# A convolution and local-attention block: image 0's first two planes as plain fp32 products, with the weight preparation around them reordered

## The reference

```
perceived = depthwise 3x3 conv (3 filters per channel) of x  + b_perc      # 384 channels
hid       = gelu(w_up1 @ perceived + b_up1)                                # 256 channels, exact gelu
h         = x + w_up2 @ hid + b_up2                                        # 128 channels
q, k, v   = w_qkv @ h + b_qkv
out       = h + sum over the 3x3 neighbourhood of softmax(q.k * 128**-0.5) * v   # zero-padded borders
```

## Time and profile before

| | |
|---|---|
| median of 3 runs | 394.77 us (394.73 to 394.92) |
| the profiled execution's own time | 394.93 us |
| span in the profile | 393.1 us, granted clock 0.999 |
| busy: PE / DVE / ACT / POOL | 382.4 / 340.3 / 256.5 / 180.0 us |
| DMA | 33.98 MB, mean 86 GB/s |

### The profile page before, as it was taken

How to read it: one execution, slowest core, us unless ns; L and a number is a source line. 1 busy time by engine, 2 the same in 40 slices (tenths; PEclk the granted TensorE clock), 3 DMA queues, 4 the chain that set the end, 5 groups by cost and what they waited for, 6 DMA issues and landing times.

```text
span 393.1 us, 10470 instructions
## 1 busy us (share of the span) xinstructions
PE 382.4 (97%) x3664; PEld 359.6 (91%) x3664; DVE 340.3 (87%) x919; ACT 256.5 (65%) x542; POOL 180.0 (46%) x159
## 2 busy tenths in 40 slices
PE   5999999999999999999999999999999999999995
PEld 4999998999989999999999999999999999999874
DVE  4999999999988889888888988888898888887795
ACT  6645478929485774848477484847748484773893
POOL 5784563646445262635525263552526355132111
PEclk9999999999999999999999999999999999999999
DMA  7420301434151513325150332515033231403003
GB/s 226 183 67 3 121 2 25 139 45 170 31 187 20 171 32 65 141 39 173 25 181 14 74 131 39 173 26 175 21 71 132 39 107 26 121 12 85 3 27 135
DMA packets 56313, 33.98 MB, mean 86 GB/s; under 512 B 47200, under 2 KB 48096, under 8 KB 56288
## 3 DMA queue, kind: packets, MB, share of 16 engines
q1 hardware_dynamic: 56000, 33.61, 30.3%
q10 hardware_dynamic: 288, 0.05, 0.1%
HBM read 19.86 MB, written 8.39 MB: 72 GB/s over the span
## 4 chain that ended last, share of the span: by engine, by line
PE 83%; DVE 11%; issue 2%; DMA 1%; ACT 1%; POOL 0%; DVEq 0%; ACTq 0%
PE m_ps L484 45%; PE work L539 10%; PE s_ps L609 9%; PE work L583 7%; PE s_ps L592 6%; PE s_ps L578 2%; PE s_ps L575 2%; PE s_ps L576 2%; DVE t L970 1%; DMA wp<-w_perc 1%; DVE tlo L977 1%; DVE h_around L1238 1%; DVE h_lo L987 1%; DVE s_ps L1012 1%; PE work L562 1%
## 5 line engine op out<-in xcount | busy, mean ns | idle before, releaser
L484 PE MATMUL m_ps<-thi,whi 128*128 128x256 f32 x558 | 158.9, 285 | 0.9 <-DVE ru_sb L1058 0.8
L484 PE MATMUL m_ps<-thi,wlo 128*128 128x256 f32 x558 | 155.5, 279 | 0.0
L484 PE MATMUL m_ps<-tlo,whi 128*128 128x256 f32 x558 | 154.3, 276 | 0.0
L484 PEld LDWEIGHTS m_ps<-thi,whi 128*128 128x128 f32 x558 | 104.8, 188 | 4.3 <-issue 1.0
L484 PEld LDWEIGHTS m_ps<-tlo,whi 128*128 128x128 f32 x558 | 105.6, 189 | 0.6
L484 PEld LDWEIGHTS m_ps<-thi,wlo 128*128 128x128 f32 x558 | 104.9, 188 | 0.0
L1404 POOL TENSOR_TENSOR hid_lo<-hid,hid_hi 128x1024 fp32r<-128x1024 f32 x30 | 72.2, 2406 | 27.9 <-ACT hid_hi L741 21.4
L1381 POOL TENSOR_TENSOR fc<-xp 128x512 f32<-128x512 f32 x16 | 21.3, 1333 | 98.3 <-DVE tlo L977 91.8
L731 ACT ACTIVATE hid<-y,b1eff 128x1024 f32<-128x1024 f32 x31 | 35.7, 1152 | 33.1 <-DVE y L1081 23.1
L715 ACT CAST thi<-t 128x1024 fp32r<-128x1024 f32 (+1 forms) x32 | 25.1, 832 | 48.6 <-DVE t L970 48.5
L807 ACT ACTIVATE p_sb<-p_sb,negmax 128x101 f32<-128x101 f32 x128 | 46.8, 369 | 6.2 <-DVE negmax L1111 6.1
(11 more groups left out here) (156 smaller groups left out, 765.6 us busy)
## 6 DMA issues: line engine op xcount, KB each, us to landing
xp<-x_planes SPq DMA_DIRECT2D x16, 640.0 KB, 5.3
xr<-x_rows SPq DMA_DIRECT2D x16, 512.0 KB, 4.1
out<-o_sb SPq DMA_DIRECT2D x28, 256.0 KB, 4.0
pt<-ptc SPq DMA_DIRECT2D x140, 32.0 KB, 1.9
pt<-ptc SPq DMA_DIRECT2D x28, 28.0 KB, 1.9
out<-y SPq DMA_DIRECT2D x3, 256.0 KB, 2.5
w1T<-w SPq DMA_DIRECT2D x1, 384.0 KB, 3.6
out<-y SPq DMA_DIRECT2D x2, 128.0 KB, 2.4
```

Of the source, the lines that this page charges most:

```text
L484: last = pe.matmul(bank[:, col + first:col + end], a[:, j, dy, half * P:(half + 1) * P], c[:, par, T_PLACE[j], first + by:end + by], start ...
```

## The change

For image 0, planes 0 and 1 of both halves are computed by plain fp32 matmuls (`whole_products`) straight from `t` and the unsplit weights: plane 0 before `small_weights`, plane 1 after it. The remaining eight units follow plane by plane in a new order (plane 5, then 3, 2, 4 for half 0, then for half 1). The three products after `small_weights` (L471) are gone, and `keep_busy` multiplies a zeroed tile instead of w1T, four times. DVE does tap column 0, then image 0's transform, then tap column 2; ACT makes the diagonals before its part of tap column 2. The low parts of weights 0 and 1, needed from image 1 on, go to POOL, the folded bias to ACT, `z_base` to image 1's body on DVE. `weff` 1 and 3 live elsewhere, and image 0 has other banks. The w1T transfer is cut in three, and image 0's planes are loaded from ACT's queue after the filters and the identity, no more from SP's after w1T. DVE makes image 1's first `tlo` part ahead of `combine(0, 0)`, the second after `finish_y(0, 0)`; POOL's `differences(2, 0)` waits until the first half's `y` of image 0 is made; the second half's `hid_lo` of image 0 is made by DVE, no more by POOL. At the end, `turn_p(n, 1)` comes after one row of copies instead of two, and one `add_h` comes after the copies.

```diff
-            sp.dma_start(w1T[:, :, :].rearrange("p m d -> p (m d)"), w1_c).then_inc(first_in, 16)
-            load_planes(0, 0)
+            for m in range(3):
+                sp.dma_start(w1T[:, m, :], w1_c[:, m * HID:(m + 1) * HID]).then_inc(w1_in[m], 16)
...
 # PE
-                    pe.matmul(work[:, 2, HID + 8:CH], w1T[:, 0, 0:P], w1T[:, 0, 8:HID], start=True, stop=True)
+                    pe.matmul(work[:, 2, S:S + WINDOW], pt[:, 0, 0, 0:P], pt[:, 0, 1, :], start=True, stop=True)
...
-                pe.wait_ge(first_in, 16)
-                keep_busy(5)
+                pe.wait_ge(zeroed, 5)
+                keep_busy(4)
+                for m in range(3):
+                    pe.wait_ge(w1_in[m], 16)
...
-                for _ in range(3):
-                    last = pe.matmul(m_ps[:, 2, S:CH], w1T[:, 0, 0:P], w1T[:, 0, 0:S], start=True, stop=True)
-                last.then_inc(warm_done, 1)
+            def whole_products(half, j, w):
+                b, col = M_PLACE[j]
+                bank = m_bank(0, half, b)
+                for k, dy in enumerate((1, 0, 2)):
+                    first, end = max(0, (1 - dy) * WIN), min(S, S + (1 - dy) * WIN)
+                    by = (dy - 1) * WIN
+                    last = pe.matmul(bank[:, col + first:col + end], w[:, dy, half * P:(half + 1) * P],
+                                     t[:, T_PLACE[j], first + by:end + by], start=(k == 0), stop=(k == 2),
+                                     skip_group_check=True)
+                return last
...
             def first_image():
...
+                pe.wait_ge(end0_done, 1)
+                pe.wait_ge(td_done, 3)
+                for half in range(2):
+                    whole_products(half, 0, end0)
+                small_weights()
+                pe.wait_ge(weff_done, 1)
+                pe.wait_ge(tp_done, 1)
+                whole_products(0, 1, weff[1])
+                pe.wait_ge(consts_done, 2)
...
+                pe.wait_ge(b1_done, 2)
+                whole_products(1, 1, weff[1]).then_inc(whole_done, 1)
                 pe.wait_ge(thi_done, 2)
                 pe.wait_ge(tlo_done, 2)
+                pe.wait_ge(wlo_dve_done, 1)
+                for half in range(2):
+                    products(0, 0, half, 5).then_inc(m_ready, 1)
                 pe.wait_ge(wlo_dve_done, 2)
+                products(0, 0, 0, 3).then_inc(m_ready, 1)
+                pe.wait_ge(wlo_dve_done, 3)
+                products(0, 0, 0, 2)
+                pe.wait_ge(wlo_dve_done, 4)
+                products(0, 0, 0, 4).then_inc(m_ready, 1)
+                products(0, 0, 1, 3).then_inc(m_ready, 1)
+                products(0, 0, 1, 2)
+                products(0, 0, 1, 4).then_inc(m_ready, 1)
...
 # image 1 on PE: before its first unit
+                if is_image(n, 1):
+                    pe.wait_ge(wlo_done, 2)
...
 # ACT
+            act.dma_start(xp[:, 0, :, :, :].rearrange("p k r w -> p (k r w)"), x_planes[0]).then_inc(x_loaded[0], 16)
...
-            for i in TAPS:
-                first_products(i)
+            first_products(0)
...
+            first_products(2)
             act.wait_ge(acc_done, 6)
-            nc.scalar.mul(whi[:, 0, :, :], tap0, -1.5).then_inc(whi_done, 1)
             nc.scalar.mul(end0, tap0, -1.5).then_inc(end0_done, 1)
...
+            for half in range(2):
+                nc.scalar.activation(b1eff[:, half:half + 1], wa[:, half:half + 1], ACT.Identity,
+                                     bias=b1[:, half:half + 1]).then_inc(b1_done, 1)
+            for k, j in ((1, 1), (2, 2), (3, 3), (4, 4)):
+                high_weights(k, j)
+            nc.scalar.mul(whi[:, 0, :, :], tap0, -1.5).then_inc(whi_done, 1)
...
 # DVE
+            sum_tap(0, 0)
+            transform_ab(0, 0)
             transform(0, 0)
             dve.wait_ge(weights_in, 16 * N_W)
             nc.vector.tensor_copy(bq_wide[:, :], bqk[:, 0:1].to_broadcast([P, P])).then_inc(bq_wide_done, 1)
+            sum_tap(1, 2)
...
-            low_weights(1, 2)
-            low_end(5, acc[2], -6.0, 3)
...
-            nc.vector.tensor_tensor(b1eff[:, :], work[:, 2, 0:2], b1[:, :], ALU.add).then_inc(b1_done, 1)
...
-            nc.vector.tensor_tensor(weff[2], sum02, acc[1], ALU.subtract).then_inc(weff_done, 1)
-            low_weights(3, 4)
+            low_weights(3, 4)
+            low_weights(2, 3)
+            low_weights(4, 5)
...
                 if is_image(n, 0):
                     transform_ab(1, 1)
                     transform(1, 1)
+                    low_t(1, 1, (0,))
                     combine(0, 0)
-                    low_t(1, 1)
                     combine_y(0, 0)
                     finish_y(0, 0)
+                    low_t(1, 1, (1,))
...
                     combine_y(1, 0)
+                    low_hid_first()
                     transform_ab(2, 0)
...
                     finish_y(1, 1)
+                    base_of_zero_keys()
...
 # DVE, the end
                 dve.wait_ge(o_ready, n * 2 - 4)
-                for row in (2, 3):
-                    place(1, row, range(0, 4))
+                place(1, 2, range(0, 4))
                 turn_p(n, 1)
-                add_h(n, 1, 1)
+                place(1, 3, range(0, 4))
                 dve.wait_ge(ptc_done, n * 2)
                 place(1, 2, range(4, 8))
+                add_h(n, 1, 1)
                 add_both_h()
...
 # POOL
             differences(1, 1)
+            for k, j, exact in ((2, 1, weff[1]), (6, 0, end0)):
+                pool.wait_ge(whi_done, k)
+                nc.gpsimd.tensor_tensor(wlo[:, j, :, :], exact, whi[:, j, :, :].bitcast(F32),
+                                        ALU.subtract).then_inc(wlo_done, 1)
...
                 if is_image(n, 0):
                     sums_ab(1)
+                    pool.wait_ge(y_part_done, 4)
                     differences(2, 0)
+                    low_query_weights()
```

More of the change, by code:

```diff
@@ L192, in build @@
         end0 = by_row(ptc[:, :, :].rearrange("p t k -> p (t k)"))
[L193 to L194 removed]
+        weff = {1: by_row(hid_flat[:, 3 * HID:6 * HID]), 3: acc[2], 2: by_row(hid_flat[:, 0:3 * HID]), 4: acc[1]}
         TAPS = (0, 2)
[L198 removed]
+        w1_in = [sem(f"w1_in{m}") for m in range(3)]
         filters_in = sem("filters_in")
@@ L343, in m_bank, with m13_of, pair_sums @@
             if is_image(n, 0):
-                return ((m_ps[:, 0, :], m_ps[:, 1, :], s_ps[:, 0, :]),
-                        (work[:, 2, :], m_ps[:, 2, :], s_ps[:, 1, :]))[half][b]
+                return ((m_ps[:, 0, :], s_ps[:, 0, :], m_ps[:, 2, :]),
+                        (work[:, 2, :], s_ps[:, 1, :], m_ps[:, 1, :]))[half][b]
+            if is_image(n, 1) and half == 0 and b == 1:
+                return work[:, 2, :]
             return m_ps[:, b, :]
+        def m13_of(n, half):
+            return q_sb[:, CH:PIX] if is_image(n, 0) and half else m13[:, :]
+        def pair_sums(n, half):
+            if is_image(n, 0) and half:
+                return o_sb[:, 0:CH], o_sb[:, CH:PIX]
+            return ps_sb[:, :], ru_sb[:, :]
         def m_count(n, half, b):
-            return 2 * b + half + 1 if is_image(n, 0) else n * 6 + (3 * half + b + 1)
+            return ((3, 4, 1), (5, 6, 2))[half][b] if is_image(n, 0) else n * 6 + (3 * half + b + 1)
         def from_image(n, base):
@@ L498, in unit @@
                 if col == 0 and half == 0 and is_image(n, 1):
-                    pe.wait_ge((m13_done, ru_done, ru_done)[b], (1, 1, 2)[b])
+                    pe.wait_ge((m13_done, m13_done, y_done)[b], (1, 2, 1)[b])
+                elif col == 0 and half and b == 1 and is_image(n, 1):
+                    pe.wait_ge(y_done, 2)
                 elif col == 0:
@@ L508, in first_image @@
             def first_image():
[L511 to L514, removed]
+                pe.wait_ge(end0_done, 1)
[7 more added lines that the diff above has]
+                pe.wait_ge(consts_done, 2)
+                pe.wait_ge(wt_copied, 2)
+                pe.wait_ge(wa_hi_done, 1)
+                pe.wait_ge(b1_done, 2)
+                whole_products(1, 1, weff[1]).then_inc(whole_done, 1)
                 pe.wait_ge(thi_done, 2)
                 pe.wait_ge(tlo_done, 2)
+                pe.wait_ge(wlo_dve_done, 1)
+                for half in range(2):
+                    products(0, 0, half, 5).then_inc(m_ready, 1)
                 pe.wait_ge(wlo_dve_done, 2)
[L518 to L533, removed]
+                products(0, 0, 0, 3).then_inc(m_ready, 1)
[6 more added lines that the diff above has]
+                products(0, 0, 1, 4).then_inc(m_ready, 1)
             def up(n):
@@ L726, in gelu @@
                 if isinstance(n, int) and n == 0:
-                    act.wait_ge(b1_done, 1)
-                if from_image(n, 1):
+                    act.wait_ge(b1_done, 2)
+                    act.wait_ge(wlo_done, 2)
+                if is_image(n, 1) and half:
+                    act.wait_ge(hlo_dve_done, 1)
```

(12 more changed lines are left out.)

98 lines of the change are left out of this document (52 added, 46 removed).

## The result

The changed kernel takes 400.84 us (median of 6 runs, 398.74 to 401.23) against 394.85 in the same session: a ratio of 1.014, interval 1.0125 to 1.0156. It is slower by 6.0; the forecast was 394.9, the range ended at 395.9. The six executions are not alike: two took 398.74 and 399.16, the other four 400.75 to 401.23, and the one with a trace is among the four. The profiled execution took 401.2 with a span of 399.4, 6.3 more than the earlier trace rows's kernel. Neither the engines' busy shares nor their order of importance show why: PE's busy time is 384.8 against 382.4. The timelines of single engines do.

A forecast was written before the change was run, and what follows sets the result against it. DVE's chain to image 1's first tlo part was taken as the bound, not PE's stream of image 0. 394.93, +0.15 at image 1's start, 0 after, -0.16 to the median gave 394.9 us; range 394.1 to 395.7, widened to 392.9 to 395.9.

The forecast's parts named there:

- the cover of `z_base`: In image 1, z_base (0.6) costs 0, covered by DVE's idle at 61.87 (0.48) and its waits for PE.
- Part 1: First loads: filters land at 3.5, DVE's tap sums start about 1.0 earlier, planes land at 6.1 (bounds 5.4, 7.4).
- sign of being wrong: At the start: a load landing after 6.9 would show the forecast wrong.
- Rival (b): Loads, slower: planes late on ACT's queue, every us after 6.1 moves the chain; at 7.2, 395.9; chance 0.12.
- Parts 2 to 4: Image 0's transform to image 1's start: DVE and POOL alternate, tlo ends at 29.7 against 29.5, +0.15.
- Part 2: Transform ahead of tap column 2: DVE stands 3.0 us for POOL, weights 2.0 late although DVE began 1.0 early.
- Part 4: Way to image 1: POOL's low part of weight 0 ends at 25.1, image 1's ab waits for it; +0.15.
- rival (a): Image 0, faster: DVE's 3.0 standing shrinks; if all, sum02 at 11.9, image 1 at 26.5, 391.8; half, 393.3; chance 0.33.
- Part 6: Image 0's outputs and image 1: PE stalls some 0.35 at unit 4; +0.15 carried through, bounds 0 and 0.6.
- Rival (d): PE's 1.2 us wait before plane 1's second half drops its clock: 2 to 3 us, 397; chance 0.04.
- Rival (c): Image 1 and the end, slower: z_base not covered (+0.6), last burst takes the extra store (+0.5), 395.9; chance 0.09.
- Parts 5 and 7: PE's 1.0 us of extra work hides in its wait for tlo; the new end changes 0 (bounds -0.4, +0.7).

The follow-up runs named there:

- a6: Changed kernel with w1T in one transfer on SP and image 0's planes still on ACT's queue: 400.89 us, ratio 1.0152.
- a3: Changed kernel with the query weights' low part ahead of POOL's y_part_done wait and the loads as before: 395.43 us, ratio 1.002.
- c1: a4 with both tap columns ahead of image 0's transform and ACT's column 2 products ahead of its diagonals: 395.78 us, ratio 1.0039.
- d1: a4 with POOL's low part of weight 0 behind image 1's first tlo, PE waiting for it before unit 4: 394.44 us, ratio 0.9994.
- a1: Changed kernel with POOL's low part of the query weights put ahead of its wait for y_part_done: 397.26 us, ratio 1.007.
- d2: Changed kernel with 18 extra PE products filling the wait ahead of image 1's unit 4: 399.87 us, ratio 1.0114.
- a5: Changed kernel with w1T still in thirds and image 0's planes behind them on SP's queue: 399.41 us, ratio 1.0114.
- a4: a3 with z_base moved on DVE ahead of the sum of h in image 1: 394.39 us, ratio 0.9994.
- b2: Kernel before with only the change's new end (second turn_p earlier, one add_h behind the copies): 394.61 us, ratio 0.9995.
- a2: Changed kernel with the loads as before (one w1T transfer, planes behind it on SP): 397.33 us, ratio 1.0078.

## Why the prediction was wrong

The mechanism that the prediction named, image 1's start set by DVE's chain, was right. Three of its terms were not: the landing of the planes, a wait that was left out, and the cover of `z_base`.

**Part 1, the landing of the planes: the term that was mis-sized.** "A transfer seems to take its turn whole" was read from two small transfers, of 13.5 and 32 KB, whose landing may be late for several reasons. Measured: `fc` at 8.22, beyond the upper bound of 7.4, and `w1T`'s last third, whose landing was given no bound, at 7.9. The prediction's own sign of being wrong, a load landing after 6.9, came true. Rival (b) had the mechanism and its slope of 1 us per us: 2.06 late, and image 1's start moved by 2.10. The Trainium skill, "DMA: Bandwidth & Descriptors", section "Queues, rings and completion order", cited there, has a DMA engine take the queues in turn by packets; the 6.1 that the prediction drew from it, or the 0.65 more of a share by bytes, does not come out in a6, where `w1T` goes as one transfer on SP's queue and the planes on ACT's (8.49).

**Parts 2 to 4 held in their mechanism.** DVE and POOL alternated with steps of 0.73 to 0.94. a3, whose planes land as the forecast assumed (`fc` 6.05), starts image 1 at 29.50 against 29.7 forecast. That this is so close is partly luck: its `sum02` starts at 14.17, not 14.85, and the way from there to image 1's start takes 15.33, not 14.85. Part 2's 3.0 of standing for POOL was too much; c1 takes it away and gains 2.1. Part 4's remark that POOL's low part of weight 0 holds up `ab` is what d1 shows; c1 also speaks against rival (a)'s price: `sum02` at 11.71 is near that rival's 11.9, yet image 1 starts at 30.52 and not at 26.5. It took DVE for the only bound, but PE and ACT were late within 2 us, ACT in an order that c1 changed too.

**Part 6 left out a wait.** It named what is queued behind POOL's new wait for `y_part_done`, namely `fc`, and stopped at the first consumer. `low_query_weights` stands three steps further on the same engine, and PE waits for it at unit 4: 1.56 instead of the 0.35 allowed there. a1 settles it: with the step moved that wait is gone, and 3.6 are gained.

**Rival (d) had the right mechanism, the wrong place and too high a price.** In the changed kernel the clock fell not before plane 1's second half but in the wait that part 6 overlooked; 2 to 3 us were named, 1.5 to 1.6 were measured (d2). Where it fell in the place named (a5, a6), DVE's chain covered it. The costly fall was a consequence of that wait, so its chance of 0.04 was tied to the wrong condition.

**Part 6, `z_base` "covered".** The cover was looked for in DVE's idle time; the cost came from POOL. Rival (c) named the uncovered step, at 0.6. By the earlier trace rows a DVE step takes 2.64 beside `hid_lo`, and `z_base` was moved to just where `hid_lo` runs. The prediction stated the rule and didn't apply it: 0.6 was the upper bound, 2.00 the measured length, 1.0 its price at the end (a3 against a4).

**Parts 5 and 7 held.** PE's extra products cost nothing that shows (a4, level with the kernel before), and the new end is worth nothing (b2).

## What to carry to other kernels

When a wait is put into an engine's list, follow every later instruction of that list until the next point where it stood idle before, and look up on the other engines who waits for each, even if the waiter doesn't read the data. A step's price is that of its new neighbours: a DVE step of 0.33 us that moves beside a POOL step of 2.4 takes 2.0. Cutting a first load in three to have its first part sooner is to be weighed against the load behind it.

## What the runs showed of the hardware

- With a load of 384 KB in three transfers all loads moved 154 GB/s in the second of 3 to 4 us, with one transfer 425 (a5, a4); the 640 KB behind it landed some 1.8 later. POOL's first `fc` lay between 5.52 and 6.16 in all seven traces with the loads as before, between 7.34 and 8.22 in the five with the new loads. The reason inside the queue is open.
- PE's idle of 2.02 to 2.04 ahead of unit 4 was followed by a granted clock of 0.50 in the changed kernel, a5 and a6, and by 1.00 throughout in a2. In a6 it was still 1.00 when PE resumed at 38.05 and fell within the next second (windows: 0.86, then 0.50). The falls of a5 and a6 near 18.4 us follow no such idle: PE's listed waits there are 0.41 at most. What decides was not settled; with the wait filled (d2) the clock kept 1.00.
- The Trainium skill, "TensorE: Matmul & The Clock Gate", Part 1, says that idleness brings the lower clock back. The changed kernel's rows agree; a2's same idle and the earlier falls of a5 and a6 show that the length of one gap doesn't decide it alone.
